# Edge tables made during the recurrent layer, and a second buffer for the edge attention's features

## What is computed

```python
# layer 0: two graph convolutions, then for p = 1..4 an LSTM over windows of p nodes; its last state replaces row p-1 of each window
for p in range(1, MAX_SKIP + 1):
    wins = h[:, :nw * p, :].reshape(Bv * nw, p, Hd)
    last = _lstm_last(Wih[p - 1], Whh[p - 1], bih[p - 1], bhh[p - 1], wins)
    h = h.at[:, jnp.arange(nw) * p + (p - 1), :].set(last.reshape(Bv, nw, Hd))
# layer 1: attention over 512 edges (src, dst), softmax over the edges of one source
e = jnp.einsum('behd,hd->beh', leaky_relu(Xq[:, src] + Xq[:, dst], 0.2), a)
e = e + jnp.log(A0[src, dst] + 1e-8)[None, :, None]
attn = exp(e - segment_max(e)[src]) / segment_sum(...)[src]
Y = segment_sum(attn[..., None] * Xv[:, dst], src);  return Y @ W_out.T
# layer 2 needs A_hat = (A + I) * deg^-1/2 on rows and columns
```

## Time and profile before

| | us |
|---|---|
| median of 3 runs | 2220.11 |
| lowest, highest | 2218.26, 2225.47 |
| profiled execution | 2217.02 |
| its span | 2215.2 |
| PE, DVE, ACT, POOL busy | 1991.8, 1269.8, 981.9, 238.1 |

### The profile page before, as it was taken

How to read it: one execution, slowest core, us unless ns; L and a number is a source line. 1 busy time by engine, 2 the same in 40 slices (tenths; PEclk the granted TensorE clock), 3 DMA queues, 4 the chain that set the end, 5 groups by cost and what they waited for, 6 DMA issues and landing times. The chain is left out here.

```text
span 2215.2 us, 33755 instructions
## 1 busy us (share of the span) xinstructions
PE 1991.8 (90%) x12342; PEld 1628.6 (74%) x12342; DVE 1269.8 (57%) x2672; ACT 981.9 (44%) x1659; POOL 238.1 (11%) x208
## 2 busy tenths in 40 slices
PE   6998999999999999999953798988988788795998
PEld 6997888888999998888842456565564676574887
DVE  7453664454455456445525665665644577774886
ACT  2544663333333333323320572635534244563785
POOL 1000000000011100110112520101100011200100
PEclk9999999999999999999985999999999999997999
DMA  3201010000000000001031222214221211001232
GB/s 110 77 0 39 0 38 1 0 0 21 18 1 0 0 0 0 1 1 76 0 130 46 67 87 92 91 49 135 77 89 56 85 59 47 12 0 41 84 95 86
DMA packets 83117, 100.20 MB, mean 45 GB/s; under 512 B 8912, under 2 KB 75088, under 8 KB 80720
## 3 DMA queue, kind: packets, MB, share of 16 engines
q1 hardware_dynamic: 83024, 98.94, 13.6%
HBM read 62.03 MB, written 33.55 MB: 43 GB/s over the span
## 5 line engine op out<-in xcount | busy, mean ns | idle before, releaser
L588 ACT ACTIVATE b_gate<-b_pG,b_bias 128x512 f32<-128x512 f32 (+1 forms) x504 | 304.1, 633 | 365.3 <-PE b_pG L54 364.7
L52 PE MATMUL b_pG<-b_xshi,b_whi 128*128 128x512 f32 (+1 forms) x1008 | 367.6, 365 | 6.0 <-DVE b_xslo L637 5.8
L53 PE MATMUL b_pG<-b_xslo,b_whi 128*128 128x512 f32 (+1 forms) x1008 | 366.9, 364 | 0.0
L54 PE MATMUL b_pG<-b_xshi,b_wlo 128*128 128x512 f32 (+1 forms) x1008 | 366.8, 364 | 0.0
L633 DVE CAST b_xshi<-HT 128x512 fp32r<-128x512 f32 (+3 forms) x144 | 59.6, 456 | 274.8 <-PE b_pG L54 274.6
L52 PEld LDWEIGHTS b_pG<-b_xshi,b_whi 128*128 128x128 f32 x1008 | 189.7, 188 | 32.9 <-DVE b_xslo L637 6.0
L54 PEld LDWEIGHTS b_pG<-b_xshi,b_wlo 128*128 128x128 f32 x1008 | 189.8, 188 | 25.7
L53 PEld LDWEIGHTS b_pG<-b_xslo,b_whi 128*128 128x128 f32 x1008 | 189.8, 188 | 25.6
L53 PE MATMUL b_pG<-b_hslo,b_whi 128*128 128x512 f32 (+1 forms) x576 | 205.1, 356 | 0.0
L54 PE MATMUL b_pG<-b_hshi,b_wlo 128*128 128x512 f32 (+1 forms) x576 | 205.1, 356 | 0.0
L52 PE MATMUL b_pG<-b_hshi,b_whi 128*128 128x512 f32 (+1 forms) x576 | 205.1, 356 | 0.0
(11 more groups left out here) (348 smaller groups left out, 4005.4 us busy)
## 6 DMA issues: line engine op xcount, KB each, us to landing
a_xt<-in_x SPq DMA_DIRECT2D x16, 512.0 KB, 6.2
h_scratch<-HT SPq DMA_DIRECT2D x4, 2048.0 KB, 9.0
l_x<-in_x SPq DMA_DIRECT2D x16, 512.0 KB, 3.9
l_w<-h_scratch SPq DMA_DIRECT2D x16, 512.0 KB, 5.0
x_scratch<-l_x SPq DMA_DIRECT2D x16, 512.0 KB, 3.3
c_x<-x_scratch SPq DMA_DIRECT2D x32, 256.0 KB, 3.9
x_scratch<-c_x SPq DMA_DIRECT2D x32, 256.0 KB, 2.7
l_x<-x_scratch SPq DMA_DIRECT2D x16, 512.0 KB, 3.8
```

Source lines behind the costliest of these rows:

```text
L52: nc.tensor.matmul(out, w_hi, x_hi, start=first, stop=False)
L53: nc.tensor.matmul(out, w_hi, x_lo, start=False, stop=False)
L54: return nc.tensor.matmul(out, w_lo, x_hi, start=False, stop=last)
L588: nc.scalar.activation(gate[s][:, g, 0:plan.n], pG[s][:, g, 0:plan.n], SIG[g], bias=bias[:, plan.p - 1, 2 * g + s:2 * g + s + 1])\
```

## The change

The block `edge_tables` is gone. Its loads are issued by SP inside the recurrent layer, as soon as the plan for p = 4 begins, its first part on DVE (`prepare`) runs in 12 pieces inside the loop of that plan, and what needs PE is done at the opening of the attention. Buffers are placed so that they don't overlap: the tables behind `HT`, where the weights of plan 3 lay, and half `b` = 0 of the recurrent inputs where the rows of the first two tiles land. DVE makes all halves of weights (before ACT and POOL). The degrees are summed along rows on 128 partitions, and POOL takes the root of one column, not of 64. The last quarters of `HT` are written after each half, not both at the end, and the first two tiles' rows are loaded before that. The attention gets two buffers for `hT_hi` and `hT_lo`, and the hand-written order changes: a tile's `turn`, halves and `linear` come in the group two before its own for all tiles, and `make_pairs` is cut 3 and 5. The diff, cut to its core:

```diff
+                sp.wait_ge(w_ready, w_count[-1])
+                sp.wait_ge(gate_mm, end.g0)
+                for t, src in tables.loads:
+                    sp.dma_start(t, src).then_inc(tables.landed, 16)
+                for n, t in late.cols.items():
+                    sp.dma_start(t, late.a[n]).then_inc(late.cols_in, 16)
                 for i in range(SPILLS):
-                    sp.wait_ge(h_ready, end.unit(i * end.its // SPILLS, end.p - 1, 1, 1) + 1)
+                    if i == 2:
+                        sp.wait_ge(gate_mm, end.gate(1, end.p - 1, 0, 1) + 4)
+                        sp.wait_ge(spilled[0], 16)
+                        for b in range(2):
+                            part = slice(b * GROWS, (b + 1) * GROWS)
+                            sp.dma_start(late.x[b][:, :, :], x[b]).then_inc(late.landed[b], 16)
+                            sp.dma_start(late.w[b][:, :, :], spill[:, :, part]).then_inc(late.landed[b], 16)
+                    sp.wait_ge(h_ready, end.unit(i // 2, end.p - 1, i % 2, 1) + 1)
...
+                    body(0)
+                    nc.gpsimd.memset(tables.mh[:, :], -0.5).then_inc(tables.root_ready, 1)
+                    pool.wait_ge(tables.root_ready, 1)
+                    pool.wait_ge(tables.deg_ready, 1)
+                    nc.gpsimd.tensor_tensor(tables.dcol[:, :], tables.deg[:, :], tables.mh[:, :], ALU.pow).then_inc(tables.root_ready, 1)
+                    body(1)
...
+                def prepare(at):
+
+                    if at == 4:
+                        sort_keys()
+                    elif at == 5:
+                        compare(0, 2)
+                    elif at == 6:
+                        compare(2, EC)
+                        degrees()
+                    elif at == 7:
+                        count_less(0, 2)
+                    elif at == 8:
+                        count_less(2, EC)
+                    elif at == 9:
+                        spread_ends()
+                    elif at == 10:
+                        permutation()
+                    elif at == 11:
+                        fold()
+                    elif at == 12:
+                        signs()
+                        scale_columns()
+                    elif at == 13:
+                        halves(tab["wqv_hi"][:, :, D:2 * D], tab["wqv_lo"][:, :, D:2 * D], tables.w_raw[:, 1])
+                        halves(tab["wl_hi"][:, :, :], tab["wl_lo"][:, :, :], tables.wl[:, :, :])
+                    elif at == 14:
+                        halves(tab["wo_hi"][:, :, :], tab["wo_lo"][:, :, :], tables.w_raw[:, 2])
+                    elif at == 15:
+                        halves(tab["wqv_hi"][:, :, 0:D], tab["wqv_lo"][:, :, 0:D], tables.wq[:, :, :])
...
+                                    if s == 0 and T == SKIPS:
+                                        prepare((it * T + t) * 2 + b)
...
-        hT_hi, hT_lo = sb("c_hThi", [P, KD, GROWS], F32R), sb("c_hTlo", [P, KD, GROWS], F32R)
+        hT_hi, hT_lo = ([sb(f"c_hT{n}{b}", [P, KD, GROWS], F32R) for b in range(2)] for n in ("hi", "lo"))
...
-                            make_pairs(5, NP)
+                            make_pairs(3, NP)
 
                 normalise(0, 0)
                 normalise(0, 1)
+                normalise(0, 2)
                 pool.wait_ge(spilled[0], 16)
                 pool.wait_ge(spilled[1], 16 * (SPILLS - 1))
-                make_pairs(0, 2)
-                normalise(0, 2)
-                make_pairs(2, 5)
+                pool.wait_ge(tables.made, ONE_HOT)
+                make_pairs(0, 3)
                 body(0)
                 with pool.Fori(1, NQ - 1) as q:
                     body(q)
...
@@ PE, group(q, m)
                 def group(q, m, end=2 * NJ):
 
+                    n = m + 2
                     for i in range(GG):
                         gather(q, m, i)
-                        if m + 1 < end:
-                            if i == 0 and m < 2:
-                                turn(q, m + 1)
+                        if m == 0:
+                            if i == 0:
+                                turn(q, 1)
                             if i == 1:
-                                linear(q, m + 1)
-                            if i % 2:
-                                project(q, m + 1, i // 2)
-                        if m + 2 < end:
-                            if i == 3:
-                                turn_back(q, m + 2)
-                            if i == GG - 1 and 0 < m < NJ:
-                                turn(q, m + 2)
-                        if i == 2 and m + 1 < end:
-                            pe.wait_ge(sem["lin_row"], NJ * q + m + 2)
+                                linear(q, 1)
+                        elif n < end:
+                            if i == 5:
+                                turn(q, n)
+                            if m == NJ and i == GG - 1:
+                                turn_linear(q, n)
+                                turn_attention(q)
+                        if m + 1 < end and i % 2:
+                            project(q, m + 1, i // 2)
                         if i and i % 2 == 0:
                             score(q, m, i // 2 - 1)
-                            if i == 2 and m + 1 < end:
-                                turn_linear(q, m + 1)
                         elif i == 0 and m > 1:
                             score(q, m - 1, GG // 2 - 1)
                             if m == NJ:
                                 add_linear(q)
-                        if m == NJ and i == GG - 2:
-                            turn_attention(q, False)
+                        if m == 0:
+                            if i == 2:
+                                turn_linear(q, 1)
+                            if i == 3:
+                                turn_back(q, 2)
+                            if i == GG - 1:
+                                turn(q, 2)
+                        elif n < end:
+                            if i == 0:
+                                turn_back(q, n)
+                            if i == 6:
+                                linear(q, n)
+                            if m < NJ and i == GG - 1:
+                                turn_linear(q, n)
...
@@ PE, opening
+                def sort_rows():
+                    for i in range(2):
+                        for c in range(EC):
+                            last = nc.tensor.matmul(pZ[0][:, i, :], tables.spread[:, i, c, :], tables.perm[:, c, :],
+                                                    start=c == 0, stop=c == EC - 1)
+                    last.then_inc(tables.products, 1)
+
+                def scale_row():
+                    nc.tensor.matmul(pE[:, 0:NODES], tables.ones[:, :], tables.scaled[0:NODES, :], start=True, stop=True)\
+                        .then_inc(tables.products, 1)
+
+                def turn_rows():
+                    pe.wait_ge(tables.rows, ROWS_KEPT)
+                    for i, row in enumerate((s_row, d_row)):
+                        for c in range(EC):
+                            last = nc.tensor.transpose(pZ[1][:, i, c * P:(c + 1) * P], row[:, c * P:(c + 1) * P], tab["ident"][:, :])
+                    last.then_inc(tables.products, 1)
+
+                def choose():
+                    pe.wait_ge(tables.made, SOURCES)
+                    nc.tensor.matmul(pZ[0][0:NODES, 0, :], tables.adj2[0:NODES, :], oh_s[0:NODES, :], start=True, stop=True)\
+                        .then_inc(tables.products, 1)
+
+                def weigh():
+                    pe.wait_ge(tables.made, PICKED)
+                    nc.tensor.matmul(pZ[0][:, 1, :], tables.ones[:, :], picked, start=True, stop=True).then_inc(tables.products, 1)
+
                 turn_back(0, 0)
+                sort_rows()
+                scale_row()
+                turn_rows()
+                choose()
                 turn(0, 0)
+                weigh()
                 linear(0, 0)
                 project(0, 0, 0)
-                pe.wait_ge(sem["lin_row"], 1)
                 turn_linear(0, 0)
+                pe.wait_ge(tables.made, HAT)
                 project(0, 0, 1)
                 turn_back(0, 1)
                 project(0, 0, 2)
                 project(0, 0, 3)
+                pe.wait_ge(tables.made, WEIGHT)
+                pe.wait_ge(tables.rows, COLS_KEPT)
                 group(0, 0)
+                linear(0, 2)
                 score(0, 0, GG // 2 - 1)
+                turn_linear(0, 2)
...
@@ ACT, opening
+                act.wait_ge(tables.products, SORTED)
+                nc.scalar.activation(s_row, pZ[0][:, 0, :], ACT.Copy).then_inc(tables.rows, 1)
+                nc.scalar.activation(d_row, pZ[0][:, 1, :], ACT.Copy).then_inc(tables.rows, 1)
+                act.wait_ge(tables.products, TURNED)
+                nc.scalar.activation(tables.s_col[:, :], pZ[1][:, 0, 0:EDGES:P], ACT.Copy).then_inc(tables.rows, 1)
```

(63 more changed lines are left out.)

444 lines of the change are left out of this document (199 added, 245 removed).

## The result

The changed kernel takes **2172.03 us** (median of 4 runs, 2165.33 to 2173.02) against 2221.51 of the kernel before in the same runs: ratio 0.9776, 95% interval 0.9756 to 0.9796. It is faster by 49.5 us; foreseen were 77.4 and 2142.7 us, and the range ended at 2164. The profiled executions took 2217.0 and 2172.95, so there the gain is 44.1 us.

| stretch | before | after | change | foreseen |
|---|---|---|---|---|
| start to the end of the last `HT` write | 1142.33 | 1153.87 | +11.5 | +0.3 |
| to the attention's first transposes | 56.0 | 1.3 | -54.7 | -54.1 |
| opening, to the first gather | 25.4 | 22.3 | -3.1 | +2.3 |
| quarter 0 | 154.7 | 163.5 | +8.8 | |
| quarter 1 | 130.4 | 127.4 | -3.0 | |

The account below looks back on a forecast made before the run. TensorE was taken as the bound, except in a 56 us unhidden stretch before the attention. Terms -54.1 + 0.3 + 2.3 - 20.7 - 4.5 - 3.8 + 3.1 = -77.4 us gave 2142.7 us on the runs' scale, range 2129 to 2164.

Parts of the forecast that it names:

- Part 1: Between last hidden state and attention's first transposes: the tables leave the stretch, a 1.9 us boundary remains, -54.1 us.
- Part 2: Last recurrent part: VectorE's 12 table pieces and SyncE's loads are covered, except half the ranks at step 0, +0.3 us.
- Part 3: Attention's opening, at the low clock as before: linear term starts at 15.6 us instead of 13.3, +2.3 us.
- Part 4 (a): Group 1 of quarters 1 to 3: a second feature buffer makes it a plain group of 17.8 us, -20.7 us.
- a plain cause that goes: Argument against the first rival: group 1's waits of 4 to 5 us have a simple cause that the change removes.
- The sign that the prediction named: Group 1 of a later quarter: no wait over 1 us in front of `c_pT` would confirm the second buffer's gain.
- (b): Seven plain attention groups: two waits of about 0.5 us remain, 18.75 us instead of 19.4, -4.5 us.
- Free, just: Quarter 0: GpSimd's five pairs end 3.4 us after tile 4's variance, its power wanted at 4.4, so no cost.
- (c): Group 4 with the softmax: 21.4 us instead of 22.7, as a product moves behind a projection, -3.8 us.
- (d): Quarter 0: tile 2 finished at group 0's end with nothing beside it, group 1 2.9 us shorter, +3.1 us.
- the first (the groups gain nothing, 2168.6): Rival for the attention's groups: VectorE's chain sets the pace, so the new order gains 0, 2168.6 us; chance 10%.
- The sentence on the port: Attention's normalising: GpSimd contends with VectorE for SBUF, the step costs 2.2 us; without it 0.8, (b) near -11.

Follow-up runs that it names:

- Experiment 1: The changed kernel with half 0's recurrent buffers moved 96 bytes lower, onto a multiple of 128: 2159.37 us, ratio 0.9723.
- experiment 2: The kernel before with 32 bytes of padding, so all eight recurrent state buffers start 32 beyond a multiple of 128: 2236.12 us, ratio 1.0068.
- Experiment 5: The kernel before with the three copies at a quarter's end issued after the last fetch of rows: 2207.77 us, ratio 0.9947.
- experiment 4: The changed kernel with SyncE's three copies at a quarter's end issued after the last fetch of rows: 2157.45 us, ratio 0.9718.
- experiment 7: The changed kernel with GpSimd's five pairs behind tile 3 split, three there and two behind tile 4: 2170.11 us, ratio 0.9766.
- experiment 8: The changed kernel with half 0's buffers on a multiple of 128, copies after the last fetch and pairs split: 2143.86 us, ratio 0.9657.
- experiment 10: On top of experiment 8, the normalising of the attention's tiles entirely on VectorE, none on GpSimd: 2157.35 us, ratio 0.9711.
- experiment 12: On top of experiment 10, GpSimd's pairs in quarter 0 wait until VectorE has ended the tile's normalising: 2127.78 us, ratio 0.9587.

## Why the prediction was wrong

The sign was right, the size was not: of the foreseen 77 us, 33 did not come in the profiled execution.

**Part 1 was right**: -54.7 against -54.1. The boundary took 1.3 us, not 1.9, and nothing waited for a landing.

**Part 2 was the first step that failed.** It asked only whether VectorE's pieces and SyncE's issues had cover, and they had: the one hole of PE is 0.43 us, near step 0 as foreseen. That half 0's buffers move to another address it did not price at all. Experiment 1 shows the address alone to be worth 12.7 us of the run, 10.9 of them in the layer, and experiment 2 shows the same on the old kernel. About 1 us more is in the part p = 4 with the good address too (294.6 against 293.6 us), where +0.3 was foreseen, and probably belongs to the tables' work.

**Part 3 erred the other way**: 22.3 us instead of 27.7. The sum was made at the low clock, "as before". In the kernel before the clock was low through the 56 us ahead of the transposes (0.50) and for most of the opening (0.62); with that stretch gone it was low only at the opening's start, 0.71 over the first 5.8 us and 1.00 from there on (0.92 over the whole), and the linear term stood at 12.6 us instead of 15.6. Here the change paid in a way that its own parts don't show.

**Part 4 (a) was the second step that failed**: -20.7 foreseen, -5.6 measured (group 1 of quarters 1 to 3: 24.7, 24.1 and 26.2 us before, 22.8, 24.0 and 22.6 after). It took the wait for `c_hTlo` to have "a plain cause that goes". I had read the releaser of PE's wait, but not what VectorE itself had waited for just before: a DMA, 4.06 us. The second buffer took tile 2 out of group 1, and the same late row stopped the projection instead. Experiment 5 shows the cause in the old kernel, experiment 4 in the new one. The length foreseen for a group 1 without the wait was right: in experiment 4 the three take 20.4 us less than before, half of it by moving the copies alone (experiment 5: 10.6). The sign that the prediction named, no wait over 1 us in front of `c_pT`, held, while 3.5 to 4.6 us stood in front of `c_pU`. **(b)** -4.5 foreseen, -0.5 measured: five plain groups are 0.4 to 0.5 us shorter (19.0, foreseen 18.75) and the one in the last quarter 1.8, but group 2 of quarter 0 is 3.5 longer. "Free, just" for GpSimd's five pairs was false. The power was taken to be wanted 4.4 us after the tile's variance; it started 2.3 us late, and PE's transposes waited 2.63 us where they wait 0.28 with the pairs out of the way (experiment 7), so there was no slack in this trace. That the last product also held VectorE's sum came on top and cost about 0.1 us here. **(c)** -3.8 foreseen, -0.4 measured: in quarter 1 the wait of 2.0 us for `c_attnlo` is gone, as foreseen, but the transposes of tile 2 wait 1.15 us for their rows in its place, and that tile's linear term is now in the group as well; no run isolates it. **(d)** +3.1 foreseen, +5.8 measured: group 0 is 8.2 longer, group 1 2.4 shorter; PE idles 2.46 us for the low halves of tile 2 and runs at the low clock around it. Some 2.8 us more are in the last group and the later layers. Most of it belongs to this one execution: behind the attention it took 461.1 us, the kernel before 458.6, and experiments 1, 4, 7 and 8 458.7 to 459.4. Of the prediction's own rivals the first (the groups gain nothing, 2168.6) came nearest in the number, but mostly by other mechanisms: the fetch and the address. VectorE's chain had a share all the same: with the normalising on VectorE alone (experiment 12) a plain group falls from 19.0 to 18.0 us, and 1.4 below the kernel before is close to the 1.6 (11 us in 7 groups) that the prediction gave for the step without GpSimd's half.

**The sentence on the port** was right and too weak. The row had 1.15 against 0.406 us. What experiments 10 and 12 add is that VectorE's product is not slowed but shut out: 1.38 us for four alone, 11.22 us beside 10.87 us of GpSimd, and up to 3.7 us for a single one, the length of one of GpSimd's. The Trainium skill says so in "SBUF — State Buffer", section "SBUF: two separate sides": of a GpSimd instruction and a VectorE instruction in a two-port mode or with two inputs in SBUF, whichever starts first holds the shared pair of ports for the whole instruction, and the other blocks fully. These traces agree. In the prediction I weighed only the word of the Trainium skill's "GPSIMD Engine Reference", contention, and so took GpSimd's half as a given; as measured, the division of the normalising between the two engines costs more (2.35 us) than VectorE alone (1.38).

## What to carry to other kernels

When a buffer moves, write down its address before and after: in the recurrent layer here a moving operand off a multiple of 128 bytes cost up to 2.8%, and a pace that changes shows as a longer stretch without a hole. When a wait is to be removed, follow the chain one engine further than its releaser, down to the DMA and to what its queue issued ahead of it; otherwise the next consumer inherits it. When an engine is given work ahead of something that another one waits for, take its slack from the trace of a group that runs as it will run: 4.4 us on paper were none. And put GpSimd's long products where VectorE has nothing to do from SBUF to SBUF, not beside it.

## What the runs showed of the hardware

- In the recurrent layer the pace of 128x512 float32 products follows the start address of the moving operand: 0.2267 us on a multiple of 128, 0.229 at 64 beyond (one run), 0.233 at 32 or 96 beyond. With 336 columns the part took 280.7 us on the multiple and at 32 and 64 beyond, 281.4 at 96. In the attention's linear term no such difference was seen (0.230 and 0.231).
- A GpSimd product of 3.6 us holds some of VectorE's instructions to its end, however short they are: a sum of 128x4 took 2.51 instead of 0.16 us, four products of 128x256 took 11.22 instead of 1.38 beside three of GpSimd's. Sums that read PSUM (the low halves, 1.22 to 1.23 us) took no longer beside it.
- The fetch of a quarter's last rows (256 KB) took 5.2 to 5.9 us from issue to landing behind 1.1 MB of copies, in both kernels, and 2.9 to 3.8 us ahead of them (experiments 4 and 5).
